# The message stage: edge weights in the one-hot matrix, plain fp32 product, nine row buffers

## The reference

```python
seg = edge_type * n + dst
agg = segment_sum(x[src], seg, N_REL * n)
mean = agg.reshape(N_REL, n, -1) / max(cnt, 1)
h1 = einsum('rni,rio->no', mean, W_rel) + x @ W_root + b_rgcn
xw = h1 @ W_gcn
out = segment_sum(xw[src] * norm[:, None], dst, n) + xw * dinv**2 + b_gcn
```

## Time and profile before

| | us |
|---|---|
| median of 3 runs | 1937.72 |
| lowest, highest | 1936.33, 1941.32 |
| span of the profiled execution | 1936.6 |
| its own time | not recorded beside the span |
| median of the runs less the span | 1.1 |
| PE busy | 1546.1 (80%) |
| DVE busy | 937.3 (48%) |
| ACT busy | 569.4 (29%) |
| POOL busy | 610.1 (32%) |
| mean TensorE clock, share of 2.4 GHz | 0.872 |

### The profile page before, as it was taken

The page is one execution under the profiler, slowest core; times in us unless marked ns, Lnnn a source line. Parts: engine busy times, 40 slices in busy tenths (PEclk is TensorE's granted clock), DMA queues, the critical chain, the costliest instruction groups (busy, mean ns, idle before and its releaser), DMA issues.

```text
span 1936.6 us, 24591 instructions
## 1 busy us (share of the span) xinstructions
PE 1546.1 (80%) x8308; PEld 1242.9 (64%) x8308; DVE 937.3 (48%) x2121; ACT 569.4 (29%) x783; POOL 610.1 (32%) x532
## 2 busy tenths in 40 slices
PE   8699968658765068975999999999747899799884
PEld 7578757645453045545999999999735565466542
DVE  5663658831430036323656656565335670348802
ACT  0811034411110000004545455554334551113220
POOL 0710377777766600002312122121034550111102
PEclk9888877868867579977999999999867899879997
DMA  7004500000041110015787777878448950225523
GB/s 183 7 0 5 101 2 1 2 1 1 3 148 26 3 27 1 1 49 203 257 293 271 276 284 272 291 260 292 162 143 274 287 193 1 89 74 181 166 94 128
DMA packets 113117, 244.43 MB, mean 126 GB/s; under 512 B 30887, under 2 KB 52584, under 8 KB 112958
## 3 DMA queue, kind: packets, MB, share of 16 engines
q1 hardware_dynamic: 76382, 137.21, 22.7%
q0 software_dynamic: 24144, 72.21, 13.5%
q10 hardware_dynamic: 12528, 34.22, 4.4%
HBM read 202.83 MB, written 45.20 MB: 128 GB/s over the span
## 4 chain that ended last, share of the span: by engine, by line
PE 50%; POOL 14%; DMA 12%; issue 10%; DVE 9%; ACT 3%; SPq 2%; POOLq 0%; DVEq 0%; ACTq 0%; PEldq 0%
PE PS L2048 23%; POOL evwb L578 5%; POOL zidxb L580 4%; PE PS L2010 4%; PE PS L2185 3%; PE PS L1809 3%; POOL edge_dram L597 3%; DMA zg<-z_dram,grow 3%; PE PS L2038 2%; PE PS L1978 2%; PE PS L1843 2%; DVE compared L1712 2%; PE PS L2196 2%; DVE compared L1713 2%; PE PS L2167 2%
## 5 line engine op out<-in xcount | busy, mean ns | idle before, releaser
L625 POOL DMA_INDIRECT xg<-xn_dram,xrow x68 | 109.8, 1614 | 440.2 <-DVEq L1170 337.6
L2048 PE MATMUL PS<-whi,xhi 128*128 128x384 f32 x840 | 221.8, 345 | 5.7 <-DVE xlo L1018 5.7
L2048 PE MATMUL PS<-whi,xlo 128*128 128x384 f32 x840 | 215.7, 337 | 0.0
L2048 PE MATMUL PS<-wlo,xhi 128*128 128x384 f32 x840 | 215.3, 337 | 0.0
L1018 DVE TENSOR_TENSOR wlo<-raw,whi 128x2304 fp32r<-128x2304 f32 x72 | 184.5, 2562 | 61.5 <-ACTq L839 48.3
L1809 PE MATMUL PS<-hot_dr,hot_s 125*125 125x512 bf16 (+9 forms) x880 | 137.1, 305 | 28.7 <-DVE hot_dr L1056 28.7
L2048 PEld LDWEIGHTS PS<-whi,xhi 128*128 128x128 f32 x840 | 149.7, 191 | 6.6 <-DVE xlo L1018 6.6
L2048 PEld LDWEIGHTS PS<-whi,xlo 128*128 128x128 f32 x840 | 153.5, 190 | 0.0
L2048 PEld LDWEIGHTS PS<-wlo,xhi 128*128 128x128 f32 x840 | 153.5, 190 | 0.0
L837 ACT ACTIVATE whi<-raw 128x2304 fp32r<-128x2304 f32 x68 | 145.1, 2134 | 22.4 <-DMA xn_dram<-xn 10.3
L1018 DVE TENSOR_TENSOR xlo<-PS,xhi 128x768 fp32r<-128x768 f32 x70 | 67.0, 958 | 132.6 <-ACTq L848 127.0
(11 more groups left out here) (374 smaller groups left out, 2662.8 us busy)
## 6 DMA issues: line engine op xcount, KB each, us to landing
raw<-in_L_gnn_W_rel SPq DMA_DIRECT2D x72, 1152.0 KB, 7.8
z_dram<-xn ACTq DMA_DIRECT2D x70, 384.0 KB, 7.3
w<-in_L_ffn_w SPq DMA_DIRECT2D x18, 576.0 KB, 5.0
y_dram<-yb ACTq DMA_DIRECT2D x17, 384.0 KB, 3.2
w2e<-in_L_ffn_w SPq DMA_DIRECT2D x9, 576.0 KB, 5.8
gw<-in_L_gnn_W SPq DMA_DIRECT2D x2, 2304.0 KB, 26.9
fw<-in_L_ffn_w SPq DMA_DIRECT2D x8, 576.0 KB, 6.4
fw<-in_L_ffn_w SPq DMA_DIRECT2D x1, 4608.0 KB
```

What stands on the lines that cost most here:

```text
L625: pool.indirect_dma_start(xg[b][j][:, :], None, xn_dram, bass.IndirectOffsetOnAxis(ap=xrow[:, b, j:j + 1], axis=0)).then_inc(x_gathered[b] ...
L2048: mm = pe.matmul(slot(q)[:, s * BANK:s * BANK + HALF], a[:, k, :], wt[:, k, s * HALF:(s + 1) * HALF], start=(k == 0 and part == 0), stop=( ...
```

## The change

In the message stage the rows aren't split any more. ScalarE has no part in it. VectorE writes for each group one fp32 matrix hotw: where the one-hot has a one, it has the weight of the edge. TensorE multiplies it, as stationary matrix, with the gathered rows as they are, in two plain fp32 products of 384 columns, after waiting for hotw and for the gather. There are nine row buffers in place of five; the gather into one waits for msg_used, the product of nine groups before. The buffers mhi and mlo 2 and 3 and hotf 2 and 3 go; the nine row buffers and four hotw are in their place, and the other branch keeps what it used. Seven semaphores of the tables become one, tables_ready, which VectorE raises by one for each table in the order of its program; each waiter waits for its table's number.

```diff
+ZRING = 9
+CIDX_TABLE, IN_ROW_TABLE, PRES_TABLE, INV_TABLE, ZROW_TABLE, EPLACE_TABLE, MORE_TABLE = range(1, 8)
...
-                zg += [sb("zg4", [128, D], f32, first)]
-                mhi += [sb(f"mhi{b}", [128, D], f32r, first) for b in (2, 3)]
-                mlo += [sb(f"mlo{b}", [128, D], f32r, first) for b in (2, 3)]
+                zg += [sb(f"zg{b}", [128, D], f32, first) for b in range(4, ZRING)]
+                hotw = [sb(f"hotw{b}", [128, P], f32, first) for b in range(4)]
+            zrows = [b[:, :] for b in zg]
...
                 for q in range(T * GT):
-                    if q >= 5:
-                        pool.wait_ge(msg_ready, q - 4)
-                    pool.indirect_dma_start(zg[q % 5][:, :], None, z_rows,
-                                            bass.IndirectOffsetOnAxis(ap=grow[:, q:q + 1], axis=0)).then_inc(gathered[q % 5], 16)
+                    if q >= ZRING:
+                        pool.wait_ge(msg_used, q - ZRING + 1)
+                    pool.indirect_dma_start(zrows[q % ZRING], None, z_rows,
+                                            bass.IndirectOffsetOnAxis(ap=grow[:, q:q + 1], axis=0)).then_inc(gathered[q % ZRING], 16)
...
             with act.Else():
-                for q in range(T * GT):
-                    act.wait_ge(gathered[q % 5], 16 * (q // 5 + 1))
-                    if q >= 4:
-                        act.wait_ge(msg_used, q - 3)
-                    act.activation(mhi[q % 4][:, :], zg[q % 5][:, :], ACT.Copy, scale=grec[:, q, 1:2]).then_inc(msg_hi, 1)
                 act.sem_inc(act_step, step.n - first_step)
...
                     if q >= 4:
                         dve.wait_ge(msg_used, q - 3)
-                    dve.tensor_scalar(hotf[q % 4][:, 0:P], iota_all[:, 0:P], grec[:, q, 2:3], None, ALU.is_equal)
-                    dve.wait_ge(msg_hi, q + 1)
-                    dve.scalar_tensor_tensor(mlo[q % 4][:, :], zg[q % 5][:, :], grec[:, q, 1:2], mhi[q % 4][:, :].bitcast(f32),
-                                             ALU.mult, ALU.subtract).then_inc(msg_ready, 1)
+                    dve.tensor_scalar(hotw[q % 4][:, :], iota_all[:, 0:P], grec[:, q, 2:3], grec[:, q, 1:2],
+                                      ALU.is_equal, ALU.mult).then_inc(msg_ready, 1)
...
                         pe.wait_ge(msg_ready, q + 1)
-                        for high, part in ((True, mhi[q % 4]), (False, mlo[q % 4])):
-                            for s in range(2):
-                                mm = pe.matmul(slot(n % 4)[0:P, s * BANK:s * BANK + HALF], hotf[q % 4][:, 0:P],
-                                               part[:, s * HALF:(s + 1) * HALF],
-                                               start=q == n * GT and high,
-                                               stop=q == (n + 1) * GT - 1 and not high, skip_group_check=True)
+                        pe.wait_ge(gathered[q % ZRING], 16 * (q // ZRING + 1))
+                        for s in range(2):
+                            mm = pe.matmul(slot(n % 4)[0:P, s * BANK:s * BANK + HALF], hotw[q % 4][:, :],
+                                           zrows[q % ZRING][:, s * HALF:(s + 1) * HALF],
+                                           start=q == n * GT, stop=q == (n + 1) * GT - 1, skip_group_check=True)
                         mm.then_inc(msg_used, 1)
```

More of the change, by code:

```diff
@@ L182, in build @@
         onehots_ready, onehots_used = sem("onehots_ready"), sem("onehots_used")
-        cnt_ready, inv_ready, inv_stored = sem("cnt_ready"), sem("inv_ready"), sem("inv_stored")
-        cidx_ready, evw_loaded, evw_ready = sem("cidx_ready"), sem("evw_loaded"), sem("evw_ready")
+        cnt_ready, inv_stored = sem("cnt_ready"), sem("inv_stored")
+        evw_loaded, evw_ready = sem("evw_loaded"), sem("evw_ready")
         idx_used = sem("idx_used")
@@ L201, in build @@
         folded, fold_used = sem("folded"), sem("fold_used")
-        pres_ready = sem("pres_ready")
+        tables_ready = sem("tables_ready")
         xn_stored, inlist_ready, rows_ready = sem("xn_stored"), sem("inlist_ready"), sem("rows_ready")
@@ L206, in build @@
         xhi_ready, xlo_ready = sem("xhi_ready"), sem("xlo_ready")
-        zrow_ready, zrow_stored, z_begun, z_filled = sem("zrow_ready"), sem("zrow_stored"), sem("z_begun"), sem("z_filled")
+        zrow_stored, z_begun, z_filled = sem("zrow_stored"), sem("z_begun"), sem("z_filled")
         ld_shared, ld_w13, ld_w2e = sem("ld_shared"), [sem(f"ld_w13_{b}") for b in range(RING)], [sem(f"ld_w2_{b}") for b in range(RING)]
@@ L221, in build @@
         act_more, dve_more, pe_more = sem("act_more"), sem("dve_more"), sem("pe_more")
-        in_row_ready, eplace_ready, cleared, grec_blank = sem("in_row_ready"), sem("eplace_ready"), sem("cleared"), sem("grec_blank")
+        cleared, grec_blank = sem("cleared"), sem("grec_blank")
         rec_stored, grec_loaded, grow_ready = sem("rec_stored"), sem("grec_loaded"), sem("grow_ready")
-        more_ready, rows_loaded = sem("more_ready"), sem("rows_loaded")
-        gathered = [sem(f"gathered{b}") for b in range(5)]
+        rows_loaded = sem("rows_loaded")
+        gathered = [sem(f"gathered{b}") for b in range(ZRING)]
         msg_hi, msg_ready, msg_used, hot_ready = sem("msg_hi"), sem("msg_ready"), sem("msg_used"), sem("hot_ready")
@@ L338, in build @@
             h1 = sb("h1", [P, T, D], f32, g)
-            hotf += [sb(f"hotf{b}", [128, P], f32r, g) for b in (2, 3)]
             with ExitStack() as first:
-                zg += [sb("zg4", [128, D], f32, first)]
-                mhi += [sb(f"mhi{b}", [128, D], f32r, first) for b in (2, 3)]
-                mlo += [sb(f"mlo{b}", [128, D], f32r, first) for b in (2, 3)]
+                zg += [sb(f"zg{b}", [128, D], f32, first) for b in range(4, ZRING)]
+                hotw = [sb(f"hotw{b}", [128, P], f32, first) for b in range(4)]
+            zrows = [b[:, :] for b in zg]
             xws = sb("xws", [P, T, D], f32, g)
@@ L406, in _ @@
             sp.dma_start(v_b[:, :], w["L0_ffn_v_b"].partition_broadcast(P)).then_inc(ld_gate, 16)
-            sp.wait_ge(inv_ready, 1)
+            sp.wait_ge(tables_ready, INV_TABLE)
             sp.dma_start(inv_dram.rearrange("(t p r) o -> p t (r o)", p=P, r=REL), inv[:, :, :]).then_inc(inv_stored, 16)
@@ L417, in _ @@
             sp.wait_ge(z_begun, 16)
-            sp.wait_ge(zrow_ready, 1)
+            sp.wait_ge(tables_ready, ZROW_TABLE)
             sp.dma_start(zrow_dram.rearrange("(t p r) o -> p t (r o)", p=P, r=REL), zrow[:, :, :]).then_inc(zrow_stored, 16)
-            sp.wait_ge(more_ready, 1)
+            sp.wait_ge(tables_ready, MORE_TABLE)
             sp.wait_ge(grec_blank, 16)
@@ L572, in _ @@
             pool.wait_ge(zrow_stored, 16)
-            pool.wait_ge(cidx_ready, 1)
+            pool.wait_ge(tables_ready, CIDX_TABLE)
             with step.turns(ET // AHEAD, 3) as j:
@@ L590, in _ @@
             pool.wait_ge(grec_blank, 16)
-            pool.wait_ge(eplace_ready, 1)
+            pool.wait_ge(tables_ready, EPLACE_TABLE)
             with step.turns(ET // AHEAD, 2) as j:
@@ L641, in further_gather @@
                                         bass.IndirectOffsetOnAxis(ap=xrow[:, 0, 0:1], axis=0)).then_inc(m_gathered, 16)
-            pool.wait_ge(more_ready, 1)
+            pool.wait_ge(tables_ready, MORE_TABLE)
             further_tiles(pool, further_gather)
@@ L905, in further_tile @@
                 act.sem_inc(begun, 1)
-            act.wait_ge(more_ready, 1)
+            act.wait_ge(tables_ready, MORE_TABLE)
             act.sem_inc(m_stored, 16)
@@ L1048, in _ @@
             do(dve.scalar_tensor_tensor(cidx[:, 0, :], ef[:, 1, :], float(REL), ef[:, 2, :], ALU.mult, ALU.add))
-            dve.sem_inc(cidx_ready, 1)
+            dve.sem_inc(tables_ready, 1)
             def onehots(j, b, first):
@@ L1081, in _ @@
             do(dve.tensor_copy(in_row[:, :], ga[:, :, ET - 1]))
-            dve.sem_inc(in_row_ready, 1)
+            dve.sem_inc(tables_ready, 1)
             dve.wait_ge(full[3], BEFORE["edges"][3] + 1)
@@ L1092, in _ @@
             do(ts(pres[:, :, :], counts[:, :, N:N + REL], 1.0, None, ALU.min))
-            dve.sem_inc(pres_ready, 1)
+            dve.sem_inc(tables_ready, 1)
             do(dve.reciprocal(inv[:, :, :], inv[:, :, :]))
-            dve.sem_inc(inv_ready, 1)
+            dve.sem_inc(tables_ready, 1)
             for t in range(T):
@@ L1136, in _ @@
             do(ts(zrow[:, :, :], further[:, :, :], 0.0, None, ALU.max))
-            dve.sem_inc(zrow_ready, 1)
+            dve.sem_inc(tables_ready, 1)
             dve.wait_ge(full[2], BEFORE["ranks"][2] + 1)
@@ L1155, in _ @@
                 do(dve.scalar_tensor_tensor(rec[:, :, 2], in_group[:, n, :], float(-n * P), rec[:, :, 2], ALU.mult, ALU.add))
-            dve.sem_inc(eplace_ready, 1)
+            dve.sem_inc(tables_ready, 1)
             def in_list(r, b):
@@ L1184, in _ @@
             do(dve.tensor_copy(more_n[:, :], ran[0:1, upto, REL - 1:REL]))
```

(6 more changed lines are left out.)

## The result

| | us | ratio to the kernel before (95%) |
|---|---|---|
| before, median of 4 | 1938.11 | |
| after, median of 4 (1956.23 to 1963.16) | 1958.28 | 1.0106 (1.0086 to 1.0125) |
| after, run again beside later kernels, median of 6 | 1954.81 | 1.0070 (1.0046 to 1.0093) |

The change makes the kernel slower, by 1.1% in the first comparison and by 0.7% in the second. 1953.1 had been forecast, in a range from 1946 to 1960. The two profiled executions differ by 21.4 us: 17.6 in the message stage, 3.5 behind it, 0.3 ahead of it.

A forecast was written before the change was run, and what follows sets the result against it. A chain in which now the transfer, now TensorE comes last was taken as the bound. Products +44.3, later weights +1.5, waits and half speed covered -30.4 gave +15.4 us: 1953.1 us, range 1946 to 1960.

The forecast's parts named there:

- The product: Message stage, TensorE: two plain fp32 products cost 1.29 us a group in place of 0.70, +44.3 us over 75 groups.
- Dense products cover the waits and the half speed: Message stage after the root weights: dense products cover TensorE's waits and its time at 1.2 GHz, -30.4 us.
- The gathers stay ahead with nine buffers: Message stage: gathers run up to nine ahead beside root products and lose little without, 12.9 us of products against 12.6.
- The first ten groups: Start of the message stage: root weights asked for 1.5 us later, used at 1461.6; the 2.1 us saved vanish.
- a sign of being right: TensorE's wait at the root weights in the message stage would still be 8 to 11 us.
- The arbitration rule: Root weights' load: DMA engines alternate between queues by packet, so earlier gathers can't delay it; wait ends nearer 1460 than 1465.
- Semaphores: Tables: seven signals become one, nobody waits for a later event and no instruction is added, 0 us.
- The sum: Message stage: the last product ends at 1608.3 against 1592.9, +15.4 us, for a total of 1953.1 us.
- the forecast's own range: Total time of 1948 to 1958 us, with root weights from 1457.8 to 1465 and a product of 0.645 to 0.65.
- The first: Rival, message stage: transfers, not TensorE, are the bound; the end comes 28 us earlier, total 1910; chance 0.04.
- The second: Rival, message stage: TensorE also starves or slows beside other weight loads; +8.5 us, total 1961.5; chance 0.13.
- The third: Rival: the wait for the root weights shrinks, TensorE starting on them 10 us earlier; within 0.3%; chance 0.05.

The follow-up runs named there:

- e4: Changed kernel with the weighted one-hot in bf16 and the product on upper half words of the gathered rows; 1908.02 us, 0.9844 of the kernel before.
- e1: Changed kernel with five row buffers in place of nine; 1961.68 us, 1.0108 of the kernel before.
- e7: The changed kernel itself, run again beside the later kernels; 1954.81 us, 1.0070 of the kernel before.
- e10: Kernel before, split kept, five row buffers, those from the fifth on in the normalised rows' tile, one semaphore for the tables; 1942.56 us, 1.0003.
- e9: Changed kernel with the product on upper half words and the root weights asked for as soon as the relations are done; 1900.80 us, 0.9786 of the kernel before.
- e2: Changed kernel with the root weights asked for as soon as the relations are done, not after six groups; 1946.89 us, 1.0044 of the kernel before.
- e3: Kernel before, split and four products kept, with nine row buffers and one semaphore for the tables; 1926.57 us, 0.9932.
- e5: Kernel before with the root weights asked for as soon as the relations are done; 1932.65 us, 0.9951.
- e8: Kernel before, split kept, with seven row buffers and one semaphore for the tables; 1926.34 us, 0.9918.
- e6: Kernel before, split kept, with nine row buffers, one semaphore for the tables and root weights as soon as the relations are done; 1916.12 us, 0.9872.

## Why the prediction was right, and where its steps were off

- **The product** (1.29 us a group in place of 0.70, +44.3 us after the weights): right. 1.297 in the stretches without root products, 2.58 with. e4 shows by itself that this is the cost.
- **Dense products cover the waits and the half speed** (-30.4): right, measured -29.0. From the root weights to the end of the last product (1462.61 to 1610.75) there are 148.1 us against 146.7 in the sum, and its terms without waits are 145.3, so of the 31.8 us of waits and half speed 2.8 are left. The half speed after the wait lasts 4.0 us (1462.61 to about 1466.6) in place of 2.7, and a block of 17 groups takes 31.9 us (1483.54 to 1515.42) in place of 31.7.
- **The gathers stay ahead with nine buffers**: right, though e1 shows that five would nearly have done.
- **The first ten groups**: right in the end only because two errors nearly cancel. The request was not 1.5 us later but 0.2, since the clock rose at 1439.3 already. And the weights took 17.95 us from request to use; before it was 15.63 (1444.48 to 1460.11). The prediction read 15.0 there and kept 15.1, which from 1446.0 gives 1461.1; its 1461.6 comes out only with 15.6. So the end of the wait, 1462.6, was missed by 1.0 us as the sum of 1.3 too late and 2.3 too short. That part is luck. TensorE's own wait was 12.8 us (12.4 in e7), more than the 8 to 11 that had been named as a sign of being right. The step said that the data in flight are the same, up to tile 18 in both, and so they are; but in the changed kernel the gathers are issued up to 7.7 us earlier, and more of them go before the weights are through. With nine buffers the weights took 17.5 to 18.6 us in four profiles, with five 13.8 to 16.0 in three, with seven 16.9.
- **The arbitration rule** of the Trainium skill (DMA: Bandwidth & Descriptors) had been read so that a deeper gather queue could not push the weights back. The runs say that it does, by 4 us for four tiles. The rule on turns isn't refuted by that: a queue of gathers that runs dry earlier would leave the weights more of the engines, which fits but was not tested. The inference from it was wrong.
- **Semaphores: nothing**: right, as far as e10 shows, with the new place of the buffers (1.0003).
- **The sum**: +15.4 forecast. The profiles have +17.6 in the stage, and the medians +20.2 and +14.3. The first comparison holds 3.5 us behind the stage for which the sum had no term; without them its 1958.28 would not have passed the upper end, 1958, of what the prediction called the forecast's own range.
- **Rivals.** The first (transfers are the bound, faster) asked for a product under 0.54 us; it cost 0.645. At 0.17, in e4, the transfers do take over, at 301 GB/s and with the wait for the weights: 140.0 us. Without that wait, in e9, it is 125.2, within the rival's 107 to 134. The second did not come: no half speed amid dense products, no starving. The third did not come either, since the wait grew; e2 shows that even without it the change is slower, by 0.44%.
- **What I had wrong without the forecast suffering**: that nine buffers bring nothing because five and four split halves are nine too. In the split kernel they bring 10 us. What counts is how many gathers are in flight, not how many tiles lie between gather and product.

## What to carry to other kernels

Before taking work off helper engines, ask what TensorE pays for it: here two passes beside each other on engines that were not full were swapped for 0.59 us a group on the engine that then became the bound, and the waits of the stage could give back only two thirds. Count buffers as transfers in flight, and measure what one takes at each number: here 5.8 us with five, 8.3 with nine, so four more buffers brought 10 us of stage and the last two of them 1. A large load that TensorE will wait for belongs ahead of the stream of small ones, best where the DMA engines are idle; behind them it pays for those in front of it. What it costs to put it ahead into full DMA engines isn't shown here.

## What the runs showed of the hardware that was not expected

Gathers on GpSimd are issued in 0.95 us in the changed kernel, every one; with VectorE's subtraction beside them some take up to 2.0. All gathers of the kernel after (min, median, max in ns), and then 40 of those of e3:

```profile
L664 POOL DMA_INDIRECT zg<-z_dram,grow x85: 941/946/1002, 1430.2 to 1590.0; - x85
```

```profile
L665 POOL DMA_INDIRECT zg<-z_dram,grow x40: 942/1000/1878, 1425.3 to 1566.7; - x40
```

Of the 85 gathers 14 took over 1.3 us in the kernel before, 16 in e10, 21 in e5 and in e8, 26 in e3, 28 in e6, and none in any kernel with the plain product. The kernel before, two subtractions and the issues beside them:

```profile
1434.67 1.02 DVE L1614 SCALAR_TENSOR_TENSOR mlo<-zg,grec,mhi 128x768 fp32r<-128x768 f32 x1 [7.20 <-ACT mhi L932]
1434.94 1.57 POOL L663 DMA_INDIRECT zg<-z_dram,grow  x1 [0.30 <-issue]
...
1437.93 1.01 DVE L1614 SCALAR_TENSOR_TENSOR mlo<-zg,grec,mhi 128x768 fp32r<-128x768 f32 x1
1438.08 1.68 POOL L663 DMA_INDIRECT zg<-z_dram,grow  x1 [0.31 <-DVE mlo L1614]
```

The issues begin 0.27 and 0.15 us after the subtractions do, and both end 0.82 us after the subtractions' ends. So it is with all 14 of this kernel: they begin 0.11 to 0.35 us into a subtraction and end 0.81 to 0.83 us after it, while 22 issues that begin 0.25 to 0.85 us ahead of a subtraction, with none running, take 0.95 us in spite of it. An issue that comes second waits until the subtraction is over; it isn't merely slowed. The Trainium skill (SBUF — State Buffer, on the two separate sides) says that VectorE operations with two SBUF inputs and GpSimd operations that read SBUF lock one pair of ports against each other. The numbers agree with it; which of the two inputs does it was not tried. What this costs the stage isn't shown.

Why the part ahead of the first gather varies by 11 us between profiles stays open.
